# Reordering the front of a delta-rule layer: keys one group ahead, the first group by tiles, the rates as four pieces, the last queries turned by GpSimd

## The chip, the cores and the metric

The kernel runs on one core of one Trainium2 chip. The metric is the device time of one launch in microseconds. It is compared before and after the change, by the median of several executions of each kernel. The profile of the kernel before is one further execution.

## The reference

A vision tower of 32 images with 64 tokens each and width 256 passes through eight layers with a layer norm behind each: patch embedding and attention, a mixture of experts, a gated delta rule with 16 heads of 16, and further mixing, attention and expert layers. The change touches the delta layer alone:

```python
q = silu(x @ Wq).reshape(b, n, h, hd)
k = silu(x @ Wk).reshape(b, n, h, hd)
k = k * rsqrt(sum(k * k, -1, keepdims=True) + 1e-12)
v = (x @ Wv).reshape(b, n, h, hd)
beta = 2.0 * sigmoid(x @ Wbet)
a = sigmoid(x @ Wf)
def step(S, inp):                       # one of n = 64 steps
    Sd = at * S
    u = vt - einsum('bhk,bhkv->bhv', kt, Sd)
    Sn = Sd + bt * kt * u
    return Sn, einsum('bhk,bhkv->bhv', qt, Sn)
```

Here x is the layer norm of the expert layer's output. The steps can't begin before the keys and rates of all images are there, since one step works on all 32 images and 16 heads at once (512 chains, on 128 partitions in four groups).

## The kernel before, in words

The 2048 tokens are 16 tiles (T) of 128; four tiles (NT), which are eight images, make a group, and there are four groups (CG). Every engine has its own program; programs meet at semaphores. What stands between the end of the expert layer and the first step is called the front here.

- **Rows.** SyncE (`sync`) loads the two expert outputs of a tile into one of four buffers (`load_rows`, L1339); VectorE (`collect`, L1570 to L1583) adds them to H and takes the statistics; GpSimd (`rstd`, L1669) finishes them; ScalarE (`norm`, L1469) writes the normed tile; TensorE turns it (`turn`, through the helper at L108) and ScalarE copies it to xT (`copy_xT`, L1476).
- **Projections.** Six pieces of 128 features (0 and 1 are the queries, 2 and 3 the keys, 4 and 5 the values) fill PSUM banks 2 to 7, each from two matmuls over the 512 tokens of a group (L1388; the first group in two halves of 256 tokens, L1398). The 32 rates are one 32x512 sum in bank 1 (`rate_sums`, L1414), which the turns of odd tiles use too. A matmul in f32 runs as two instructions in the trace. ScalarE evicts with Silu or Copy (`made_of`, L1487) and the rates with Tanh (`rates_of`, L1497).
- **Change of layout.** Tokens lie along the free axis, but the steps need one chain to a partition: each piece is stored to DRAM (`store_made`, L1325, 1024 runs of 256 bytes) and a whole group of queries, keys or values is loaded back (`load_chain`, L1331). Keys and rates go and come by SyncE's queue; queries and values are stored by ScalarE's queue and loaded by GpSimd's.
- **Keys.** ScalarE squares a group of keys (`square_keys`, L1501), VectorE takes their norms by Newton steps and makes the scaled keys `ka` (`sum_keys`, `scale_keys`, L1595 to L1618), GpSimd makes `kb` (L1678). ScalarE turns the queries to time order (`turn_queries`, L1505).
- **Order.** TensorE and ScalarE follow `ticks`: a step with a lag of so many tiles, once per tile or per group. Per group TensorE does keys, rates, values, queries, one pair beside one turn. All stores and loads of keys on SyncE's queue stand behind all row loads. GpSimd takes the groups in order: values, queries, then `kb` of that group ahead of the next loads.
- **Steps.** Their program (L1635 on) begins when all pieces are stored, `kb` is made four times, the queries are turned, TensorE has cleared the states (L1454) and ScalarE has placed the values of the first step (L1508), which follows a load of its activation table. The 64 steps then run at VectorE's pace.

Of the kernel before, what the change touches and what calls it, by code (L numbers as in the profile page):

```python
# [16 lines left out]
F32 = mybir.dt.float32  # L17
# [1101 lines left out]
def vit_rest(nc, io, banks, H, ident, ident_bf, minus_half, const, const_in, scores_all, top, which, gate, xn_rows,  # L1119
             token_rows, spare):  # L1120
    chains = {n: nc.dram_tensor(f"chains_{n}", (CG, P, HD * TOK), F32).ap() for n in "qkvo"}
    rates = nc.dram_tensor("rates", (CG, 2, IMAGES // CG, HEADS, TOK), F32).ap()
    inter = nc.dram_tensor("inter", (T * GPT, ME, D), F32).ap()
# [112 lines left out]
def delta_front_buffers(nc, ctx):  # L1236

    def sb(name, shape, dt=F32):
        return ctx.enter_context(nc.sbuf_tensor(name, shape, dt))

    ng = IMAGES // CG * TOK
    return {"w": sb("w_delta", [P, DC, 3 * D]), "w_rate": sb("w_rate", [P, DC, 2 * HEADS]), "ys": sb("ys", [P, YS, 2, D]),
            "stats": [sb(f"stats_d{p}", [P, 6]) for p in range(2)], "agg": sb("agg_d", [P, T, 2]),
            "shift": sb("shift_d", [P, T]),
            "xT": [sb(f"xT_d{p}", [P, DC, ng]) for p in range(2)], "made": sb("made", [P, 6, ng]),
            "rate_made": sb("rate_made", [2 * HEADS, ng])}

# [14 lines left out]
def delta_layer(nc, sem, io, banks, H, ident, minus_half, token_rows, gate, chains, rates, front, chain, all_sent,  # L1262
# [50 lines left out]
    def rate_bank():  # L1313
        return banks[0:2 * HEADS, 1, :]

    def ticks(steps, last):
        for tick in range(last):
            for lag, per, count, step in steps:
                if tick >= lag and (tick - lag) % per == 0 and (tick - lag) // per < count:
                    step((tick - lag) // per)  # L1320

# [16 lines left out]
    def sync(sp):  # L1338
        def load_rows(t):  # L1339
            sp.dma_start(ys[t % YS][:, :, :], token_rows[0:2 * T * P, :]  # L1340
                         .rearrange("(k t p) d -> t p k d", k=2, p=P)[t]).then_inc(sem(f"ys{t % YS}"), 16)

        def next_rows(t):
            sp.wait_ge(sem("added"), t + 1)
            load_rows(t + YS)

        def send_keys(g):
            store_made(sp, g, 2)
            store_made(sp, g, 3)
            sp.wait_ge(sem("rate_made"), g + 1)  # L1350
            for kind in range(2):
                sp.dma_start(rates[g, kind, :, :, :].rearrange("b h t -> h b t"),
                             rate_made[kind * HEADS:(kind + 1) * HEADS, :].rearrange("h (b t) -> h b t", t=TOK)
                             ).then_inc(sem("rate_stored"), 16)
            load_chain(sp, g, "k", k)
            sp.wait_ge(sem("rate_stored"), 32 * g + 32)
            for kind in range(2):
                sp.dma_start(rate[:, g, kind, :], rates[g, kind, :, :, :].rearrange("b h t -> (b h) t")
                             ).then_inc(sem(f"rates{g}"), 16)

        all_sent(sp)
        for t in range(YS):
            load_rows(t)
        for t in range(T - YS):
            next_rows(t)
        for g in range(CG):
            send_keys(g)
        for g in range(CG):
            sp.wait_ge(sem(f"normed_o{g}"), 1)
            sp.dma_start(chains["o"][g], o[:, g, :, :].rearrange("p d t -> p (d t)")).then_inc(stored_o[g], 16)  # L1370

    def tensor(pe):
        def turn(t):
            if t >= 2:
                pe.wait_ge(sem("xT_copied"), t - 1)
            if t % NT == 1 and t > NT:
                pe.wait_ge(sem("rate_made"), t // NT)
# [3 lines left out]
        def project(first):  # L1381
            def step(g):
                pe.wait_ge(sem("xT_copied"), NT * g + NT)
                for m in (first, first + 1):
                    if g:
                        pe.wait_ge(sem(f"made{m}"), g)
                    for c in range(DC):
                        ins = pe.matmul(banks[:, 2 + m, :], w[:, c, m * P:(m + 1) * P], xT[g % 2][:, c, :],  # L1388
                                        start=(c == 0), stop=(c == 1))
                    ins.then_inc(sem(f"sums{m}"), 1)  # L1390
            return step

        def project_half(half, pieces):
            at = slice(half * NT // 2 * P, (half + 1) * NT // 2 * P)
            pe.wait_ge(sem("xT_copied"), (half + 1) * NT // 2)
            for m in pieces:
# [3 lines left out]
                if half:  # L1400
                    ins.then_inc(sem(f"sums{m}"), 1)

        def first_half(_):
            project_half(0, (2, 3, 4, 5, 0, 1))

        def second_half(first):
            def step(g):
                if g:
                    project(first)(g)
                else:  # L1410
                    project_half(1, (first, first + 1))
            return step

        def rate_sums(g):  # L1414
# [21 lines left out]
        def sum_squares(n, part):  # L1436
# [9 lines left out]
        ticks([(1, 1, T, turn), (3, 1, 1, first_half), (5, 4, CG, second_half(2)), (5, 4, CG, rate_sums),  # L1446
               (6, 4, CG, second_half(4)), (7, 4, CG, second_half(0))], T + 4)
        pe.wait_ge(sem("zeroed"), 1)
# [19 lines left out]
    def scalar(act):  # L1468
# [5 lines left out]
        def copy_xT(t):  # L1474
            act.wait_ge(sem("xT_made"), t + 1)
            g, i = t // NT, t % NT  # L1476
            if g >= 2 and i == 0:
                act.wait_ge(sem("sums5"), g - 1)
            act.copy(xT[g % 2][:, :, i * P:(i + 1) * P], turned_bank(t)).then_inc(sem("xT_copied"), 1)

        def made_of(first, func):
            def step(g):
                for m in (first, first + 1):
                    act.wait_ge(sem(f"sums{m}"), g + 1)
                    if g:
                        act.wait_ge(sem(f"stored{m}"), 16 * g)
                    act.activation(made[m][:, :], banks[:, 2 + m, :], func).then_inc(sem(f"made{m}"), 1)  # L1487
                if first != 2:
                    for m in (first, first + 1):
                        store_made(act, g, m)  # L1490
            return step

        def rates_of(g):
            act.wait_ge(sem("rate_sums"), g + 1)
            if g:
                act.wait_ge(sem("rate_stored"), 32 * g)
            act.activation(rate_made[:, :], rate_bank(), ACT.Tanh, scale=0.5).then_inc(sem("rate_made"), 1)  # L1497
# [21 lines left out]
        def square_out(n):  # L1519
            act.wait_ge(sem("o_made"), CUTS[n + 1])  # L1520
            if n:
# [3 lines left out]

        ticks([(0, 1, T, norm), (1, 1, T, copy_xT), (5, 4, CG, made_of(2, ACT.Silu)), (5, 4, CG, rates_of),
               (6, 4, CG, made_of(4, ACT.Copy)), (7, 4, CG, made_of(0, ACT.Silu)), (9, 4, CG, square_keys),
               (12, 4, CG, turn_queries)], T + 9)
        act.preload_act_table_set("natural_log_exp_and_others")
# [37 lines left out]
    def vector(dve):  # L1567
# [39 lines left out]
        def scale_keys(g):  # L1607
            dve.wait_ge(sem(f"rates{g}"), 32)
            once.mark(dve.tensor_scalar(rate[:, g, 1, :], rate[:, g, 1, :], 0.5, 0.5, ALU.mult, ALU.add))
# [23 lines left out]
        dve.wait_ge(sem("kb_made"), CG)  # L1633
        dve.wait_ge(sem("q_turned"), CG)
        dve.wait_ge(sem("values_placed"), 2)  # L1635
# [14 lines left out]
        for h in range(2):  # L1650
            dve.wait_ge(sem(f"state{h}"), TOK + 1)
        once.mark(dve.tensor_tensor(prod[:, :, :, 0:HD], S[TOK % 2], bcast(qt[:, last, :, :], 2, HD), ALU.mult))
        once.settle()
# [13 lines left out]
    def gpsimd(pool):  # L1667
# [16 lines left out]
        prepare(pool)  # L1684
        for g in range(CG):
            if g:
# [904 lines left out]
def laid_out_more(inputs, a, rows, wide, tok):  # L2591
# [12 lines left out]
    def columns(v):  # L2604
# [37 lines left out]
        "delta_w": rows(np.concatenate([a("L1_attn_Wq"), a("L1_attn_Wk"), a("L1_attn_Wv")], 1)),  # L2642
        "rate_w": rows(np.concatenate([a("L1_attn_Wbet"), a("L1_attn_Wf")], 1)),
        "delta_o_w": rows(a("L1_attn_Wo")),
# [82 lines left out]
```

## Time and profile before

| | us |
|---|---|
| median of 3 runs | 1377.79 (1375.93 to 1379.68) |
| the profiled execution's own time | 1378.83 |
| its span | 1377.2 |
| first collect of the front | 572.11 |
| first instruction of the steps (VectorE, L1640) | 659.93 |

TensorE is busy for 84% of the span, VectorE for 58%, ScalarE for 43% and GpSimd for 38%. These shares are means over very different stages. The front is 87.8 us long, and what counts in it is the chain of waits that ends at 659.93. In the rows further down, a line of the timeline has its start, its duration, the engine, the line of the kernel and the operation, and in brackets the engine's idle time before it and what ended that. "issue" there means that the engine's own sequencer was occupied.

### The profile page before, as it was taken

To read this page: it belongs to the slowest core of one execution; us is meant where nothing else is said; L and a number is where in the kernel's file an instruction comes from. 1 tells how busy PE (TensorE), PEld (TensorE's weight loads), DVE (VectorE), ACT (ScalarE), POOL (GpSimd) and SP (SyncE) were. 2 spreads that over 40 slices of the span, in tenths; PEclk is the share of its full clock that TensorE was granted. 3 is DMA by queue.
4 is the path that set the end of the run, shared out by engine and by line. 5 is a ranking of instruction groups with operands and counts; after the bars stand their busy time and mean duration, and the time that the engine had idled before them with its cause. 6 is when DMAs were issued, how large, how long until landed. Compare 5 with 4: busy or idle time off the path is not lost. (4 is left out here: it accounts for less than half of the span.)

```text
span 1377.2 us, 24939 instructions
## 1 busy us (share of the span) xinstructions
PE 1162.9 (84%) x9227; PEld 893.3 (65%) x9227; DVE 803.7 (58%) x1850; ACT 587.3 (43%) x1468; POOL 521.5 (38%) x565
## 2 busy tenths in 40 slices
PE   6999985699999999688689999994899999777854
PEld 4666663598999999543355656563677777655533
DVE  3666665321212121465899999994576776422886
ACT  2445542211121212155677777771244444334554
POOL 0111111232333323343688888882121222020657
PEclk9999996799999999899899999996899999878975
DMA  4111100799888887388000000002000040037601
GB/s 138 44 47 37 43 13 12 290 333 374 318 331 315 331 313 291 105 205 217 5 1 1 1 1 1 1 1 80 10 12 9 13 188 1 1 117 249 184 19 58
DMA packets 83353, 162.26 MB, mean 118 GB/s; under 512 B 44128, under 2 KB 62176, under 8 KB 77216
## 3 DMA queue, kind: packets, MB, share of 16 engines
q1 hardware_dynamic: 55536, 111.23, 23.6%
q0 software_dynamic: 10512, 45.10, 8.6%
q10 hardware_dynamic: 17184, 4.33, 1.5%
q8 instruction: 75, 1.23, 0.4%
q14 instruction: 46, 0.38, 0.1%
HBM read 134.28 MB, written 26.35 MB: 117 GB/s over the span
## 5 line engine op out<-in xcount | busy, mean ns | idle before, releaser
L922 PE MATMUL banks<-rowsT,w_up 128*128 128x128 f32 x1716 | 199.4, 276 | 0.0
L922 PEld LDWEIGHTS banks<-rowsT,w_up 128*128 128x128 f32 x1716 | 196.3, 193 | 0.1
L1431 PEld LDWEIGHTS banks<-ys,ident 128*128 128x128 f32 x1008 | 127.7, 191 | 99.8 <-POOL ys L1700 65.8
L1697 POOL TENSOR_TENSOR ys<-xT_d,q_by_time 128x1024 f32<-128x1024 f32 x63 | 149.2, 2368 | 42.6 <-ACT xT_d L1513 42.6
L1431 PE MATMUL banks<-ys,ident 128*128 128x64 f32 x1008 | 136.3, 291 | 21.8 <-POOL ys L1700 21.7
L1422 PE MATMUL banks<-made,ident 128*128 128x512 f32 x256 | 136.9, 617 | 14.5 <-DVE made L1645 14.4
L1542 ACT ACTIVATE banks<-banks,rate 128x256 f32<-128x256 f32 x256 | 104.0, 444 | 69.1 <-DVE made L1640 68.7
L936 PE MATMUL banks<-w_down,hT 128*128 128x256 f32 x468 | 107.5, 379 | 0.6 <-DVE res L1101 0.6
L1091 DVE TENSOR_TENSOR hT<-banks,silu 64x128 f32<-64x128 f32 x39 | 11.0, 283 | 165.6 <-ACT silu L979 165.6
L1643 DVE TENSOR_REDUCE banks<-made 128x32 f32<-128x544 f32 x128 | 93.2, 728 | 4.4
L864 POOL DMA_DIRECT2D w_down<-in_down_w x39 | 22.8, 585 | 186.5 <-PE banks L936 178.4
L936 PEld LDWEIGHTS banks<-w_down,hT 128*128 128x128 f32 x468 | 85.9, 190 | 11.0 <-issue 1.0
L1842 POOL TENSOR_TENSOR agg_b<-agg_b,minus_half 128x1 f32<-128x1 f32 x48 | 28.5, 593 | 170.0 <-DVE agg_b L2060 168.9
L1640 DVE TENSOR_TENSOR made<-banks,ka 128x512 f32<-128x512 f32 x128 | 87.6, 684 | 6.5 <-PE banks L1422 3.9
L1645 DVE TENSOR_TENSOR made<-kb,banks 128x512 f32<-128x512 f32 x128 | 88.0, 687 | 4.4
L1700 POOL TENSOR_TENSOR ys<-ys 128x512 f32<-128x512 f32 x63 | 79.3, 1258 | 4.9
L969 ACT COPY rowsT<-banks 128x256 f32<-128x256 f32 x39 | 14.5, 373 | 146.6 <-PE banks L108 146.6
L1513 ACT COPY xT_d<-banks 128x512 f32<-128x512 f32 x126 | 73.2, 581 | 0.0
L1101 DVE COPY res<-banks 128x256 f32<-128x256 f32 x39 | 16.6, 425 | 75.2 <-PE banks L936 75.2
L462 PE MATMUL banks<-w_tok,patches 128*128 128x256 f32 x192 | 51.2, 405 | 7.1 <-DMA patches<-in_patches 7.1
L2460 POOL TENSOR_TENSOR agg<-agg,minus_half 128x1 f32<-128x1 f32 x48 | 31.5, 657 | 60.6 <-DVE agg L2513 60.5
L454 POOL TENSOR_TENSOR ss<-ss,minus_half 128x1 f32<-128x1 f32 x16 | 8.8, 549 | 117.0 <-DVE ss L712 117.0
(313 smaller groups left out, 2350.5 us busy)
## 6 DMA issues: line engine op xcount, KB each, us to landing
w_up<-in_up_w SPq DMA_DIRECT2D x39, 1408.0 KB
w_down<-in_down_w POOLq DMA_DIRECT2D x39, 768.0 KB, 5.6
inter<-res_x SPq DMA_DIRECT2D x16, 512.0 KB, 3.1
back<-inter SPq DMA_DIRECT2D x15, 512.0 KB, 4.2
patches<-in_patches SPq DMA_DIRECT2D x16, 384.0 KB, 3.3
f<-in_f SPq DMA_DIRECT2D x6, 1024.0 KB, 10.7
ys<-token_rows SPq DMA_DIRECT2D x16, 256.0 KB, 2.8
xn_rows<-xn_all SPq DMA_DIRECT2D x16, 128.0 KB, 1.7
```

What stands on the lines that cost most here:

```text
L462: ins = pe.matmul(X, patches[t % SLOTS_IN][:, c, :], w_tok[:, c, :], start=(c == 0), stop=(c == PC - 1), skip_group_check=True)
L922: ins = pe.matmul(out[:, m * P:(m + 1) * P], w[:, c, m * P:(m + 1) * P], x[:, c, :], start=(c == 0), stop=(c == 1))
L936: ins = pe.matmul(Y, hT[j % 2][:, c, :], w_down[j % DEEP][:, c, :], start=(c == 0), stop=(c == FULL))
L1422: pe.matmul(S[(t + 1) % 2][:, halves[h], :, :], ident[:, :], outer[:, halves[h], :, :], start=False, stop=True, skip_group_check=True).the ...
L1431: ins = pe.matmul(o_sum[t % 2], ident[:, :], products[t % 2][:, :, :, n], start=(n == 0), stop=(n == FOLDED - 1))
L1513: act.copy(Sc[n % 2][:, halves[h], :, :], S[n % 2][:, halves[h], :, :]).then_inc(sem("state_copied"), 1)
L1542: ins = act.activation(S[(t + 1) % 2][:, g, :, :].rearrange("p v k -> p (v k)"), S[t % 2][:, g, :, :].rearrange("p v k -> p (v k)"), ACT.Copy,
L1640: dve.tensor_tensor(prod[:, at, :, 0:HD], S[t % 2][:, at, :, :], bcast(ka[:, t, at, :], 2, HD), ALU.mult).then_inc(sem(f"prod_made{h}"), 1)
L1643: dve.tensor_reduce(u[:, at, :], prod[:, at, :, :], AX.X, ALU.add).then_inc(sem(f"u_made{h}"), 1)
L1645: dve.tensor_tensor(outer[:, at, :, :], bcast(kb[:, t, at, :], 2, HD), bcast(u[:, at, :], 3, HD), ALU.mult).then_inc(sem(f"outer_made{h}"), 1)
L1697: pool.tensor_tensor(qs[:, :, :, :], Sc[(t + 1) % 2][:, :, :, :], bcast(qt[:, t, :, :], 2, HD), ALU.mult).then_inc(sem("qs_made"), 1)
L1700: pool.tensor_tensor(qs[:, :, :, 0:FOLDED], qs[:, :, :, 0:FOLDED], qs[:, :, :, FOLDED:2 * FOLDED], ALU.add).then_inc(sem("qs_folded"), 1)
```

## The change

What it does, engine by engine:

- **Order.** `ticks` is gone; TensorE's and ScalarE's orders are written out. TensorE: turn 0, turn 1, tile 0, turn 2, tile 1, turn 3, tile 2, turn 4, tile 3, turns 5 to 7, rates 0, keys 1, turns 8 and 9, piece 4 of group 1, turn 10, piece 5 of group 1, turn 11, rates 1, keys 2, turn 12, queries 1, rates 2, piece 4 of group 2, turns 13 and 14, piece 5 of group 2, turn 15, keys 3, rates 3, queries 2, values 3, queries 3.
- **First group.** Each of its four tiles is projected by itself (128 tokens, 24 matmul instructions) as soon as it is turned.
- **ScalarE.** Its end runs: copy 15, values 2, turn queries 0, keys 3, square keys 2, rates 3, queries 2, values 3, turn queries 1, queries 3, square keys 3, turn queries 2. `values(g)` still stores pieces 4 and 5 from ScalarE's queue.
- **Rates.** Their sum is four pieces of 32 rows and 128 columns, on partitions 0, 32, 64 and 96, so the eviction is 128x128 in place of 32x512. One store and one load for a group take the place of two and two.
- **SyncE.** The row loads of tiles 4 to 13 come first, then the keys of group 0, then the last two row loads. It stores the queries now, and loads the values and queries of group 3.
- **GpSimd.** It loads the other values and queries between the `kb` of the groups, and turns the queries of group 3 itself.

```diff
+        def store_rates(g):
             sp.wait_ge(sem("rate_made"), g + 1)
...
+            sp.dma_start(rates[g].rearrange("(b j) h n t -> (j h n) b t", b=2),
+                         rate_made[:, :].rearrange("p (b t) -> p b t", b=2)).then_inc(sem("rate_stored"), 16)
...
+        for t in range(10):
             next_rows(t)
-        for g in range(CG):
-            send_keys(g)
+        store_pair(keys, 0)
+        next_rows(10)
+        next_rows(11)
+        store_pair(queries, 0)
+        store_rates(0)
+        load_chain(sp, 0, "k", k)
+        load_rates(0)
+        store_pair(keys, 1)
...
+        store_pair(keys, 3)
+        store_rates(3)
+        store_pair(queries, 2)
+        load_chain(sp, 3, "k", k)
+        load_rates(3)
+        store_pair(queries, 3)
+        load_chain(sp, 3, "v", v)
+        load_chain(sp, 3, "q", q)
...
+        def project_tile(t):
+            at = slice(t * P, (t + 1) * P)
+            pe.wait_ge(sem("xT_copied"), t + 1)
+            for m in (2, 3, 4, 5, 0, 1):
...
+        def rate_sums(g, copied):
+            pe.wait_ge(sem("xT_copied"), copied)
+            if g:
+                pe.wait_ge(sem("rate_made"), g)
             for c in range(DC):
-                ins = pe.matmul(rate_bank(), w_rate[:, c, :], xT[g % 2][:, c, :], start=(c == 0), stop=(c == 1))
+                images = xT[g % 2][:, c, :].rearrange("p (b j t) -> p j b t", b=2, j=NT)
+                for j in range(NT):
+                    rows = slice(2 * HEADS * j, 2 * HEADS * (j + 1))
+                    ins = pe.matmul(rate_bank()[rows, :].rearrange("p (b t) -> p b t", b=2), w_rate[:, c, :],
+                                    images[:, j, :, :], start=(c == 0), stop=(c == 1), skip_group_check=True)
...
-        for g in range(CG):
-            if g:
-                scale_keys(g - 1)
-            load_chain(pool, g, "v", v)
-            load_chain(pool, g, "q", q)
-        scale_keys(CG - 1)
-        pool.wait_ge(sem("q_turned"), CG)
+        load_chain(pool, 0, "v", v)
+        load_chain(pool, 0, "q", q)
+        load_chain(pool, 1, "v", v)
+        scale_keys(0)
+        load_chain(pool, 1, "q", q)
+        scale_keys(1)
+        load_chain(pool, 2, "v", v)
+        scale_keys(2)
+        load_chain(pool, 2, "q", q)
+        scale_keys(3)
+        pool.wait_ge(sem(f"chain_q{CG - 1}"), 16)
+        pool.tensor_copy(qt[:, :, CG - 1, :].rearrange("p t d -> p d t"), q[:, CG - 1, :, :]
+                         ).then_inc(sem("last_turned"), 1)
```

## Rows read from the trace of the kernel before

**Rows 1.** Windows view: busy time and instructions per engine, granted clock, DMA share.

```profile
core 0: us, PE busy (x) PEld busy (x) DVE busy (x) ACT busy (x) POOL busy (x), PEclk, DMA share, GB/s
580.00:585.00 5.00, 5.00 (x16) 4.06 (x16) 4.62 (x15) 1.46 (x3) 2.61 (x7) 0.62 0.53 151
600.00:605.00 5.00, 4.54 (x8) 2.03 (x9) 0.61 (x3) 1.93 (x5) 3.16 (x7) 0.66 0.85 221
645.00:650.00 5.00, 4.22 (x11) 1.56 (x9) 2.99 (x7) 3.43 (x3) 3.73 (x1) 1.00 1.04 269
```

**Rows 2.** Timeline of TensorE in the front: start, duration, first to last group.

```profile
579.94 7.26 PE L1398 MATMUL banks<-xT_d,w_delta 128*128 128x256 f32 x24
...
600.46 0.41 PE L108 MATMUL banks<-ident,H 128*128 128x128 f32 x2 [2.97 <-ACT H L1471]
600.71 5.32 PE L1388 MATMUL banks<-xT_d,w_delta 128*128 128x512 f32 x8
605.96 1.90 PE L1416 MATMUL banks<-xT_d,w_rate 128*32 128x512 f32 x4
...
638.82 7.13 PE L1388 MATMUL banks<-xT_d,w_delta 128*128 128x512 f32 x16
```

**Rows 3.** Timeline of ScalarE: first copy, its stall, and the end of the front.

```profile
577.60 0.37 ACT L1479 COPY xT_d<-banks 128x256 f32<-128x256 f32 x1
...
599.72 0.60 ACT L1471 ACTIVATE H<-H,shift_d,agg_d 128x256 f32<-128x256 f32 x1 [1.53 <-issue]
...
637.10 0.60 ACT L1487 ACTIVATE made<-banks 128x512 f32<-128x512 f32 x1 [1.12 <-PE banks L1388]
...
646.00 0.60 ACT L1487 ACTIVATE made<-banks 128x512 f32<-128x512 f32 x1 [1.12 <-PE banks L1388]
...
648.82 1.06 ACT L1501 ACTIVATE chain_o<-chain_k 128x1024 f32<-128x1024 f32 x1
655.83 2.00 ACT L1505 COPY q_by_time<-chain_q 128x1024 f32<-128x1024 f32 x1 [5.95 <-DMA chain_q<-chains_q]
657.84 1.28 ACT L1529 ACT_TABLE_LOAD   x1
659.13 0.39 ACT L1508 COPY made<-chain_v 128x32 f32<-128x32 f32 x2
```

**Rows 4.** Timeline of VectorE: first and last collect, keys of group 3, first step.

```profile
600.53 0.15 DVE L1583 TENSOR_SCALAR agg_d<-agg_d 128x1 f32<-128x1 f32 x1
...
649.91 1.87 DVE L1595 TENSOR_REDUCE n<-chain_o 128x64 f32<-128x1024 f32 x1 [1.87 <-ACT chain_o L1501]
...
655.47 1.94 DVE L1618 TENSOR_TENSOR ka<-chain_k,f 128x1024 f32<-128x1024 f32 x1
659.93 0.69 DVE L1640 TENSOR_TENSOR made<-banks,ka 128x512 f32<-128x512 f32 x1 [2.52 <-ACT made L1508]
```

**Rows 5.** Timeline of GpSimd: the last load of queries, `kb`, the first product.

```profile
650.76 0.55 POOL L1331 DMA_DIRECT2D chain_q<-chains_q  x1
655.64 3.87 POOL L1678 TENSOR_TENSOR kb<-chain_k,f 128x1024 f32<-128x1024 f32 x1 [4.33 <-DVE f L1616]
668.78 2.35 POOL L1697 TENSOR_TENSOR ys<-xT_d,q_by_time 128x1024 f32<-128x1024 f32 x1 [9.28 <-ACT xT_d L1513]
```

**Rows 6.** Timeline of SyncE's issues for the last keys.

```profile
636.00 2.09 SPq L1325 DMA_DIRECT2D chains_k<-made  x2
...
643.51 0.34 SPq L1331 DMA_DIRECT2D chain_k<-chains_k  x1
```

**Rows 7.** TensorE's groups by shape: count | busy us, mean ns | idle before.

```profile
L922 PE MATMUL banks<-rowsT,w_up 128*128 128x128 f32 x1716 | 199.4, 276 | 0.0
...
L936 PE MATMUL banks<-w_down,hT 128*128 128x256 f32 x468 | 107.5, 379 | 0.6 <-DVE res L1101 0.6
...
L255 PE MATMUL banks<-w_qkv,hT 128*64 128x128 f32 x256 | 18.4, 288 | 0.0
...
L2311 PE MATMUL banks<-back,perm_t 128*32 128x256 f32 x128 | 12.0, 452 | 9.6 <-issue 8.2 <-DMA back<-inter 1.4
```

More of the change, by code:

```diff
@@ L1121, in vit_rest @@
     chains = {n: nc.dram_tensor(f"chains_{n}", (CG, P, HD * TOK), F32).ap() for n in "qkvo"}
-    rates = nc.dram_tensor("rates", (CG, 2, IMAGES // CG, HEADS, TOK), F32).ap()
+    rates = nc.dram_tensor("rates", (CG, IMAGES // CG, HEADS, 2, TOK), F32).ap()
     inter = nc.dram_tensor("inter", (T * GPT, ME, D), F32).ap()
@@ L1313, in rate_bank @@
     def rate_bank():
[L1314 to L1320, printed above, removed]
+        return banks[:, 1, 0:P]
     def store_made(queue, g, m):
@@ L1345, in next_rows, with store_pair, load_rates @@
             load_rows(t + YS)
-        def send_keys(g):
-            store_made(sp, g, 2)
-            store_made(sp, g, 3)
+        def store_pair(first, g):
+            store_made(sp, g, first)
+            store_made(sp, g, first + 1)
+        def store_rates(g):
             sp.wait_ge(sem("rate_made"), g + 1)
[L1351 to L1359, printed above, removed]
+            sp.dma_start(rates[g].rearrange("(b j) h n t -> (j h n) b t", b=2),
+                         rate_made[:, :].rearrange("p (b t) -> p b t", b=2)).then_inc(sem("rate_stored"), 16)
+        def load_rates(g):
+            sp.wait_ge(sem("rate_stored"), 16 * g + 16)
+            sp.dma_start(rate[:, g, :, :].rearrange("p n t -> p (n t)"),
+                         rates[g].rearrange("b h n t -> (b h) (n t)")).then_inc(sem(f"rates{g}"), 16)
+        queries, keys = 0, 2
         all_sent(sp)
@@ L1363, in sync @@
             load_rows(t)
-        for t in range(T - YS):
+        for t in range(10):
             next_rows(t)
-        for g in range(CG):
-            send_keys(g)
+        store_pair(keys, 0)
[6 more added lines that the diff above has]
+        store_pair(keys, 1)
+        store_rates(1)
+        load_chain(sp, 1, "k", k)
+        load_rates(1)
+        store_pair(keys, 2)
+        store_rates(2)
+        store_pair(queries, 1)
+        load_chain(sp, 2, "k", k)
+        load_rates(2)
+        store_pair(keys, 3)
[6 more added lines that the diff above has]
+        load_chain(sp, 3, "q", q)
         for g in range(CG):
@@ L1375, in turn, with turn_past_rates, project @@
                 pe.wait_ge(sem("xT_copied"), t - 1)
-            if t % NT == 1 and t > NT:
-                pe.wait_ge(sem("rate_made"), t // NT)
             pe.wait_ge(sem("ln_done"), t + 1)
             transposes(pe, turned_bank(t), H[:, t, :], ident[:, :], DC).then_inc(sem("xT_made"), 1)
[L1381 to L1384, printed above, removed]
-                    if g:
[L1386 to L1396, printed above, removed]
+        def turn_past_rates(t, g):
+            pe.wait_ge(sem("rate_made"), g + 1)
+            turn(t)
+        def project(m, g):
+            pe.wait_ge(sem("xT_copied"), NT * g + NT)
+            if g:
+                pe.wait_ge(sem(f"made{m}"), g)
+            for c in range(DC):
+                ins = pe.matmul(banks[:, 2 + m, :], w[:, c, m * P:(m + 1) * P], xT[g % 2][:, c, :],
+                                start=(c == 0), stop=(c == 1))
+            ins.then_inc(sem(f"sums{m}"), 1)
+        def project_tile(t):
+            at = slice(t * P, (t + 1) * P)
+            pe.wait_ge(sem("xT_copied"), t + 1)
+            for m in (2, 3, 4, 5, 0, 1):
                 for c in range(DC):
@@ L1399, in project_half @@
                                     start=(c == 0), stop=(c == 1), skip_group_check=True)
-                if half:
+                if t == NT - 1:
                     ins.then_inc(sem(f"sums{m}"), 1)
[L1403 to L1414, printed above, removed]
-            for c in range(DC):
-                ins = pe.matmul(rate_bank(), w_rate[:, c, :], xT[g % 2][:, c, :], start=(c == 0), stop=(c == 1))
+        def rate_sums(g, copied):
+            pe.wait_ge(sem("xT_copied"), copied)
+            if g:
+                pe.wait_ge(sem("rate_made"), g)
+            for c in range(DC):
+                images = xT[g % 2][:, c, :].rearrange("p (b j t) -> p j b t", b=2, j=NT)
[3 more added lines that the diff above has]
+                                    images[:, j, :, :], start=(c == 0), stop=(c == 1), skip_group_check=True)
             ins.then_inc(sem("rate_sums"), 1)
@@ L1445, in tensor @@
         pe.wait_ge(sem("weights"), 32)
-        ticks([(1, 1, T, turn), (3, 1, 1, first_half), (5, 4, CG, second_half(2)), (5, 4, CG, rate_sums),
-               (6, 4, CG, second_half(4)), (7, 4, CG, second_half(0))], T + 4)
+        turn(0)
+        turn(1)
+        project_tile(0)
+        turn(2)
+        project_tile(1)
+        turn(3)
+        project_tile(2)
+        turn(4)
+        project_tile(3)
+        turn(5)
+        turn(6)
+        turn(7)
+        rate_sums(0, 8)
+        project(2, 1)
+        project(3, 1)
+        turn(8)
+        turn_past_rates(9, 0)
+        project(4, 1)
+        turn(10)
+        project(5, 1)
+        turn(11)
+        rate_sums(1, 12)
+        project(2, 2)
+        project(3, 2)
+        turn(12)
+        project(0, 1)
+        project(1, 1)
+        rate_sums(2, 12)
+        project(4, 2)
+        turn_past_rates(13, 2)
+        turn(14)
+        project(5, 2)
+        turn(15)
+        project(2, 3)
+        project(3, 3)
+        rate_sums(3, 16)
+        project(0, 2)
+        project(1, 2)
+        project(4, 3)
+        project(5, 3)
+        project(0, 3)
+        project(1, 3)
         pe.wait_ge(sem("zeroed"), 1)
@@ L1476, in copy_xT, with evict, queries, keys @@
             g, i = t // NT, t % NT
-            if g >= 2 and i == 0:
-                act.wait_ge(sem("sums5"), g - 1)
-            act.copy(xT[g % 2][:, :, i * P:(i + 1) * P], turned_bank(t)).then_inc(sem("xT_copied"), 1)
[L1481 to L1491, printed above, removed]
+            if t == 2 * NT:
+                act.wait_ge(sem("rate_sums"), 1)
+            if t == 3 * NT:
+                act.wait_ge(sem("rate_sums"), 2)
+                act.wait_ge(sem("sums1"), 2)
+            act.copy(xT[g % 2][:, :, i * P:(i + 1) * P], turned_bank(t)).then_inc(sem("xT_copied"), 1)
+        def evict(first, g, func):
+            for m in (first, first + 1):
+                act.wait_ge(sem(f"sums{m}"), g + 1)
+                if g:
+                    act.wait_ge(sem(f"stored{m}"), 16 * g)
+                act.activation(made[m][:, :], banks[:, 2 + m, :], func).then_inc(sem(f"made{m}"), 1)
+        def queries(g):
+            evict(0, g, ACT.Silu)
+        def keys(g):
+            evict(2, g, ACT.Silu)
+        def values(g):
+            evict(4, g, ACT.Copy)
+            store_made(act, g, 4)
+            store_made(act, g, 5)
         def rates_of(g):
@@ L1524, in square_out @@
                        o[:, :, :, CUTS[n]:CUTS[n + 1]]).then_inc(sem("o_squared"), 1)
-        ticks([(0, 1, T, norm), (1, 1, T, copy_xT), (5, 4, CG, made_of(2, ACT.Silu)), (5, 4, CG, rates_of),
-               (6, 4, CG, made_of(4, ACT.Copy)), (7, 4, CG, made_of(0, ACT.Silu)), (9, 4, CG, square_keys),
-               (12, 4, CG, turn_queries)], T + 9)
+        norm(0)
+        norm(1)
+        copy_xT(0)
+        norm(2)
+        copy_xT(1)
+        norm(3)
+        copy_xT(2)
+        norm(4)
+        copy_xT(3)
+        norm(5)
+        copy_xT(4)
+        norm(6)
+        keys(0)
+        copy_xT(5)
+        norm(7)
+        copy_xT(6)
+        copy_xT(7)
+        values(0)
+        rates_of(0)
+        queries(0)
+        norm(8)
+        norm(9)
+        keys(1)
+        copy_xT(8)
+        copy_xT(9)
+        norm(10)
+        norm(11)
+        copy_xT(10)
+        norm(12)
+        copy_xT(11)
+        values(1)
+        rates_of(1)
+        norm(13)
+        norm(14)
+        keys(2)
+        square_keys(0)
+        norm(15)
+        copy_xT(12)
+        rates_of(2)
+        queries(1)
+        copy_xT(13)
+        copy_xT(14)
+        square_keys(1)
+        copy_xT(15)
+        values(2)
+        turn_queries(0)
+        keys(3)
+        square_keys(2)
+        rates_of(3)
+        queries(2)
+        values(3)
+        turn_queries(1)
+        queries(3)
+        square_keys(3)
+        turn_queries(2)
         act.preload_act_table_set("natural_log_exp_and_others")
@@ L1607, in scale_keys @@
         def scale_keys(g):
-            dve.wait_ge(sem(f"rates{g}"), 32)
+            dve.wait_ge(sem(f"rates{g}"), 16)
             once.mark(dve.tensor_scalar(rate[:, g, 1, :], rate[:, g, 1, :], 0.5, 0.5, ALU.mult, ALU.add))
```

12 lines of the change are left out of this document (7 added, 5 removed).

## The prediction

> **What bounds the kernel now.** I read the page's shares first and set them aside, since the change touches one stage. Then I read the windows of that stage [rows 1], the timelines of TensorE and ScalarE [rows 2, 3], those of VectorE and GpSimd [rows 4, 5], SyncE's issues [rows 6] and TensorE's groups by shape [rows 7]. The reader is to see four things.
>
> VectorE has added and measured all 16 tiles by 600.68 [rows 4], but TensorE starts the keys of group 1 at 600.71 only, and the last query sums are evicted from 646.00 [rows 2, 3]. So after 600 TensorE's queue is the bound of the front, not the rows or the norms.
>
> That queue holds waste. The clock is at its lower level for much of 580 to 585 (0.62 granted, of which 1.2 GHz would be 0.50) and again in 600 to 605 (0.66) [rows 1]. The second spell follows an idle time of 2.97 us that ended in a norm of ScalarE, and ScalarE itself had stood 1.53 us at "issue" behind its two stores of queries [rows 2, 3]. Eight instructions took 5.32 us there; sixteen took 7.13 later, 3.57 for eight [rows 2].
>
> Behind TensorE comes a tail. The sums of the last keys are evicted at 637.10; store and load bring them back for the squares at 648.82 [rows 3, 6]; VectorE works from 649.91, GpSimd's `kb` runs from 655.64 to 659.51, and the steps begin at 659.93 [rows 4, 5].
>
> A second tail ends in the same 0.5 us: the last queries land at 655.83, ScalarE turns them for 2.00, loads its table for 1.28 and places values until 659.52 [rows 3].
>
> What follows the first step is unchanged, at VectorE's pace, so I carry any shift of 659.93 to the end at full size.
>
> **The change, part by part.**
>
> *First group by tiles.* The first copy to xT ends at 577.97 [rows 3]; TensorE then works on tile 0, where before it began two tiles at 579.94 [rows 2]. Four tiles are 4 x 24 = 96 instructions of 128x128. The expert layer's same shape took 199.4/1716 = 0.116 us each [rows 7], so 11.1 us, and a turn costs 0.25 (600.46 to 600.71) [rows 2], three of them 0.8. If the clock rises when it did before (0.62 over 5 us is 3.8 us at the lower level, until 583.8) [rows 1], the 5.8 us from 577.97 do 2.9 us of that work. The remaining 9.0 end at 592.8. Turns 5 to 7, with two copies of 0.37 that they wait for, make it 594.1.
>
> *Rates in four pieces.* Before, four instructions of 128x512 took 1.90 us [rows 2]. Now there are 16 of 128 columns for each group, on four column blocks of 32. The trace has no such instruction. One bound is no overlap at all: 16 x 0.116 = 1.9. The other comes from the 32-column form L2311, 12.0/128 = 0.094 for 256 columns, or 0.047 for 128: 0.75. The 64-column form L255 gives 18.4/256 = 0.072, hence 1.15 [rows 7]. Both forms run below what a serial instruction of their length takes, so blocks do overlap. I take 1.0, between the latter two, which saves 0.9 per group. The Trainium skill (TensorEngine Tiling (Array Packing), Key Properties and Theoretical Speedup) says that column tiles load weights and multiply independently, up to four times as fast, while a change of mode drains the engine. A full factor of four would make the sum of a group about 0.5 and the end 0.5 x 4 = 2 us earlier; the trace's 32-column row shows well under 4, against 107.5/468 = 0.23 for a full 256-column instruction (0.094 against 0.23 is 2.4 times at most) [rows 7].
>
> The eviction goes from 32x512 (about 0.6) to 128x128, and one store and one load of rates go per group. All of it is beside TensorE's work: nothing on the path. A dearer rates transfer (below 1 us either way) would hide behind the keys' own, whose load is later.
>
> *Keys one group ahead.* Rates 0 end at 595.1 and the keys of group 1 start there, against 600.71: 5.6 us earlier. Beyond that, the slow spell (5.32 - 3.57 = 1.75 us) is gone if the clock stays up; TensorE's longest wait in the new order is about 0.7 us.
>
> From there to the last sum stand 18 pieces at 1.72 (the spacing of evictions, 0.60 + 1.12) [rows 3], 31.0; three rates, 3.0; eight turns, 2.0; and the copies behind turns 11 and 15, which the next sum needs whole, 0.45 each, with 0.3 for the rest: 37.2. The last query sums are there at 632.3, against 646.00. The last keys have rates 3 and six pieces behind them, 11.3 us, so they are there at 621.0, against 637.10: 16.1 us earlier.
>
> *The tail after it.* Store and load took 637.10 to 643.51 and 643.51 to 648.82, 11.7 us in all [rows 3, 6]. So the last keys are back at 632.7. ScalarE has `queries(3)` ahead of the squares: evicted from 632.3 and done at about 632.9, squares end at 633.9 (632.3 + 1.6). From the squares' end (649.88) to the first step it was 10.05 us [rows 3, 4]; the first step is then at 643.95.
>
> *SyncE's queue.* The stores of queries move from ScalarE to SyncE, eight issues; on ScalarE the pairs of groups 1 to 3 go as well as that of group 0. In front of the last keys' load stand the queries of group 2: evicted until 621.0 + 1.0 + 3.4 + 0.6 = 626.0, when the keys' store is not yet down (621.0 + 6.4 = 627.4). So the added wait costs nothing by 1.4 us. Ahead of it, the queries of group 0 hold the load of keys 0 by some 2 us; their squares stand behind keys 2 on ScalarE anyway.
>
> *Moved row loads.* The loads of tiles 14 and 15 follow the first keys' eviction (about 591) and land before VectorE comes to tile 14 at 597: nothing. Bounds: 0 to 1.8 us on the last norms, which ScalarE now runs after 605.
>
> *Last queries on GpSimd.* A copy of 128x1024 isn't in its rows. Bounds are 1.06 (ScalarE's square of that size) and 3.87 (`kb`, also with a permuted output) [rows 3, 5]; I take 2.35, as for its product of 128x1024. The queries of group 3 land at about 643.5, and GpSimd's first product came 8.85 us after the first step [rows 4, 5]. Even 3.87 is hidden; with it gone from ScalarE, 2.0 us leave the second tail.
>
> *What is late next.* Two chains stand close. GpSimd loads the queries of group 2 only after `kb` 2. Squares 0 follow keys 2, about 609.6; VectorE needs 7.5 us a group (649.91 to 657.41), so `kb` 2 ends near 634.1; load 0.6 and 5.1 to land, turn 2.0, table 1.28, values 0.39: 643.6. VectorE's four groups alone give `kb` 3 at 641.7. So a still faster TensorE would bring under 1 us more.
>
> **Sum.** 659.93 - 643.95 = 16.0 us. I take off 2.0. ScalarE still issues the stores of values 0 in the middle of the front, where a pair stalled it 1.53 [rows 3], and the last keys' return and the queries' eviction now meet to 0.1 us, so that any lateness of either counts. The gain forecast is 14.0 us. The profiled execution took 1378.83, which gives 1364.8; the median of the runs shown is 1.04 lower, which gives 1363.8. I predict 1364.3.
>
> **Rivals.**
>
> *R1, the transfers become the bound.* The DMA engines' share is 0.85 to 1.04 already in such windows [rows 1]; the same bytes now have to move in 14 us less. For: the last keys' way has two transfers in a row with no slack. Against: the bytes near the end are spread, as the queries of group 2 go earlier than values 3. If each landing is 2 to 4 us later, the first step is 4 to 8 later than 643.95 plus part of the 2.0: gain 6 to 10, 1368 to 1372.
>
> *R2, more than the sum.* The clock rises 1 to 2 us earlier and the stall of 2.0 doesn't come: gain 16 to 18, where the chain of queries 2 ends it: 1360 to 1362.
>
> *R3, slower: the clock stays low.* The waits behind turns 7, 11 and 15 and short matmuls might let the clock fall as after the 2.97 us. The price: work at the lower level takes twice its time. All of the 37.2 us from the keys of group 1 on would add 37.2 and make it 21 us slower, 1400; it decides from 16 us of such work. Against it: from 645 to 650 TensorE stood 0.78 us and the clock was granted at 1.00 [rows 1]; the fall came after it had stood 2.97 [rows 2].
>
> *R4, the change doesn't do what it says.* The reordering could move the end of TensorE's queue but not the first step, where stored pieces, values and the table gate it: within 4 us of before.
>
> **Numbers.** Forecast (gain 11 to 16) 0.67; R1 0.19; R2 0.07; R3 0.03; R4 0.04. What a measurement can tell from no change is about 0.3%, 4.1 us. Faster by more: 0.67 + 0.19 + 0.07 = 0.93. Within: 0.04. Slower: 0.03. The range reaches from R2's middle to R1's middle: 1360.5 to 1371.
>
> **What would show it.** Right: TensorE's keys of group 1 near 595 at full clock; last sums near 632 to 634; the first step near 646, with VectorE, GpSimd and ScalarE all ready within 2 us; rates at 0.8 to 1.2 us. Wrong: a granted clock below 0.9 after 595 (R3); squares of group 3 that wait on the keys' landing by over 2 us (R1); a first step that is held by ScalarE's values while `kb` is long done; or steps that run slower than before.

## The result and the profile after

| | before | after |
|---|---|---|
| median, 11 runs each (us) | 1378.42 (1373.52 to 1384.47) | 1367.94 (1361.27 to 1376.49) |
| ratio | | 0.9924 (0.9900 to 0.9948) |
| profiled execution (us) | 1378.83 | 1373.86 |
| front: first collect to first step (us) | 87.82 | 74.70 |
| first step to last store of o (us) | 287.2 | 287.2 |
| behind that, to the end (us) | 430.1 | 435.6 |

The change is 10.5 us faster (7 to 14 by the interval); 1364.3 was predicted and the range held. The front of the profiled execution is 13.1 us shorter, against 14.0 forecast. What doesn't fit is behind it: there the changed code is the same and this execution was 5.5 us slower. The experiments come back to that.

TensorE's timeline of the changed kernel, columns as in [rows 2]:

```profile
580.73 5.18 PE L1414 MATMUL banks<-xT_d,w_delta 128*128 128x128 f32 x24
...
596.75 0.65 PE L1427 MATMUL banks<-xT_d,w_rate 128*32 128x128 f32 x16 [0.46 <-ACT xT_d L1534]
597.33 3.70 PE L1405 MATMUL banks<-xT_d,w_delta 128*128 128x512 f32 x8
...
622.69 0.64 PE L1427 MATMUL banks<-xT_d,w_rate 128*32 128x128 f32 x16
623.26 10.57 PE L1405 MATMUL banks<-xT_d,w_delta 128*128 128x512 f32 x24
```

The front began at 574.74 here (572.11 before), so subtract. The keys of group 1 start 22.6 us into the front (28.6 before), the last keys' sums are there at 47.9 (65.0), the last sums at 59.1 (73.8). Of the two low-clock spells of [rows 1] the second is gone (1.00 granted from 600 to 605, 0.66 before); the first is still there (0.50 from 580 to 585). ScalarE's and GpSimd's ends of the front:

```profile
628.23 0.26 ACT L1558 ACTIVATE rate_made<-banks 128x128 f32<-128x128 f32 x1
...
635.05 0.60 ACT L1541 ACTIVATE made<-banks 128x512 f32<-128x512 f32 x1 [0.56 <-DMA chains_q<-made]
638.45 1.06 ACT L1562 ACTIVATE chain_o<-chain_k 128x1024 f32<-128x1024 f32 x1 [1.49 <-DMA chain_k<-chains_k]
643.03 1.94 ACT L1566 COPY q_by_time<-chain_q 128x1024 f32<-128x1024 f32 x1 [3.53 <-DMA chain_q<-chains_q]
```

```profile
637.91 0.58 POOL L1325 DMA_DIRECT2D chain_q<-chains_q  x1
...
645.28 3.82 POOL L1792 TENSOR_TENSOR kb<-chain_k,f 128x1024 f32<-128x1024 f32 x1 [6.79 <-DVE f L1729]
649.06 1.91 POOL L1810 COPY q_by_time<-chain_q 128x1024 f32<-128x1024 f32 x1
```

From 635 to its last turn, every idle time of ScalarE ends in a DMA, where [rows 3] had TensorE. SyncE's queue, and windows with the DMA share in the column before the last (columns as in [rows 1]; the first row is the whole front before, the second the whole front after):

```profile
624.09 1.28 SPq L1319 DMA_DIRECT2D chains_k<-made  x2
628.51 0.36 SPq L1347 DMA_DIRECT2D rates<-rate_made  x1
629.00 1.32 SPq L1319 DMA_DIRECT2D chains_q<-made  x2
630.41 2.01 SPq L1325 DMA_DIRECT2D chain_k<-chains_k  x1
```

```profile
572.11:659.93 87.82, 62.63 (x176) 30.50 (x176) 54.38 (x148) 42.90 (x71) 37.13 (x47) 0.89 0.75 192
574.74:649.44 74.70, 57.21 (x272) 33.48 (x272) 54.35 (x149) 38.51 (x70) 34.55 (x46) 0.89 0.85 226
...
625.00:630.00 5.00, 5.00 (x13) 2.28 (x12) 3.44 (x2) 2.68 (x5) 3.73 (x3) 1.00 1.14 331
630.00:635.00 5.00, 3.83 (x9) 1.33 (x7) 4.49 (x17) 2.55 (x2) 0.87 (x1) 1.00 1.13 280
```

In windows of 5 us the share is 0.92 or more from 595 to 640. The last keys' load took 8.0 us from issue to squares, 5.3 before [rows 3, 6]. The difference in landing is larger still: before, the load had landed 4.3 us after its issue (647.85), and ScalarE came to the squares 1.0 us later, behind its turn of queries 2; after, it took 8.0 to land. The share around the two was 1.04 [rows 1] and 1.13. The first step is at 649.44, released by `kb`, 9.93 us behind the end of the squares (10.05 before).

### The profile page after: what moved, and what is told of

Read it like the earlier page. It is cut to its first block and busy times, and to the rows that moved or that the text cites. A ratio compares the mean times of both kernels' runs of the same rounds, so it can differ in the third digit from the quotient of the medians.

```text
span 1372.2 us, 25136 instructions
## 1 busy us (share of the span) xinstructions
PE 1168.4 (85%) x9323; PEld 904.7 (66%) x9323; DVE 803.3 (59%) x1850; ACT 582.3 (42%) x1467; POOL 519.2 (38%) x564
## 5 line engine op out<-in xcount | busy, mean ns | idle before, releaser
L922 PE MATMUL banks<-rowsT,w_up 128*128 128x128 f32 x1716 | 202.5, 279 | 1.9 <-DMA w_up<-in_up_w 1.9
L922 PEld LDWEIGHTS banks<-rowsT,w_up 128*128 128x128 f32 x1716 | 199.2, 196 | 2.2 <-DMA w_up<-in_up_w 2.1
L864 POOL DMA_DIRECT2D w_down<-in_down_w x39 | 22.6, 579 | 190.8 <-PE banks L936 182.7
```

Source lines behind the costliest of these rows:

```text
L922: ins = pe.matmul(out[:, m * P:(m + 1) * P], w[:, c, m * P:(m + 1) * P], x[:, c, :], start=(c == 0), stop=(c == 1))
```

## The experiments

A front is read from one profile each, a time from 4 to 12 runs. The changed kernel's own two fronts differ by 0.7 us. "Load" is the issue of the last keys' load, "squares" the start of their squares, both in us from the first collect; "landed" is the time from that issue to the landing. "Held by" names what released the first step; in before, `kb` and the values ended within 0.02 us of each other. Ratios are to the kernel before on the same chip.

| kernel | load | landed | squares | TensorE's last sum | front | held by | ratio (interval) |
|---|---|---|---|---|---|---|---|
| before | 71.40 | 4.3 | 76.71 | 73.84 | 87.82 | values | |
| after | 55.67 | 8.0 | 63.71 | 59.09 | 74.70 | kb | 0.9924 (0.9900, 0.9948) |
| again | 55.37 | 7.6 | 63.00 | 59.14 | 73.99 | kb | 0.9890 (0.9858, 0.9922) |
| rates3_first | 54.76 | 10.0 | 64.74 | 58.61 | 75.73 | kb | 0.9925 (0.9900, 0.9950) |
| scalar_turn | 56.32 | 7.2 | 63.59 | 58.75 | 76.06 | values | 0.9904 (0.9875, 0.9933) |
| scalar_stores | 54.56 | 6.0 | 62.97 | 60.38 | 73.96 | kb | 0.9890 (0.9857, 0.9923) |
| light | 55.67 | 6.1 | 61.82 | 59.11 | 73.10 | values | 0.9903 (0.9873, 0.9932) |
| late_v2 | 54.65 | 6.4 | 61.10 | 58.47 | 74.22 | values | 0.9901 (0.9869, 0.9934) |
| halves | 58.27 | 6.7 | 65.03 | 61.81 | 78.81 | values | 0.9903 (0.9873, 0.9933) |
| whole_rates | 57.72 | 6.1 | 63.98 | 63.46 | 74.98 | kb | 0.9928 (0.9900, 0.9956) |
| pool_turns | 56.10 | 4.9 | 61.06 | 59.06 | 72.05 | kb | 0.9896 (0.9863, 0.9930) |
| pool_turns_ss | 54.02 | 5.4 | 61.23 | 60.10 | 72.24 | kb | 0.9900 (0.9869, 0.9930) |
| before_rates4 | 68.01 | 3.9 | 72.22 | 69.34 | 83.42 | kb | 0.9980 (0.9959, 1.0001) |
| order_only | 61.53 | 6.6 | 68.15 | 65.73 | 80.89 | values | 0.9947 (0.9925, 0.9969) |

**again**: no edit.

> The changed kernel once more. In its first profile the front (first collect of VectorE to first step) took 74.70 us against 87.82 before, 13.1 shorter, while the span from the first step on was 5.5 us longer (mean granted clock 0.84 against 0.86 in the last layers). Theory N (what is outside the front is the spread of executions): the front is 74 to 75.5 again, the steps to the last store of o 287.2 again, and the stretch behind them lies anywhere from 428 to 437 with its granted clock, so the time differs from the kernel before by 10 to 15 us. Rival S (the earlier front systematically costs something later): the stretch behind the last store of o is again 435 or more.

The front is 73.99, the stretch behind the last store of o 429.5 in place of 435.6, the median 1363.76 against 1378.58. Over the 14 profiles that stretch, whose code nobody touched, lies between 424.5 and 435.6, with no order by kernel (424.7 in scalar_stores, 430.1 before). So the 5.5 us are spread and not a price of the change; theory N holds. Slower runs go in the main with a lower clock: of the changed kernel's 11, those at a mean grant of 0.927 took 1361.27 and 1363.81, that at 0.916 took 1373.86 and that at 0.877 took 1376.49.

**rates3_first**

```diff
-        square_keys(2)
         rates_of(3)
+        square_keys(2)
```

> ScalarE's order alone: the last rates are evicted before the squares of group 2. In the changed kernel they waited behind those squares until 628.23, SyncE stood at their store (624.09 + 1.28 to 628.51), and the load of the last keys was issued at 630.41 and took 8.0 us to the squares. Theory Q (SyncE's queue held by the rates makes the last keys late): the store of rates goes at about 625.5, the load of keys is issued about 1 us earlier, the front is 0.5 to 1.5 us shorter. Rival D (the DMA engines are full, share 1.13 there, so the landing is set by bytes in flight): the keys land at the same time within 0.4 us, and the front stays at 74.7.

The load left 0.6 to 0.9 us earlier and its keys were squared 1.0 to 1.7 us later, 9.98 us after the issue. Leaving earlier bought nothing, which is against Q. D is missed too: it had the landing within 0.4 us and the front at 74.7, and both came 1 us or more later (75.73). This is one profile, and why the load took 10.0 us stays open.

**scalar_turn**

```diff
-        pool.tensor_copy(qt[:, :, CG - 1, :].rearrange("p t d -> p d t"), q[:, CG - 1, :, :]
...
+        turn_queries(3)          # on ScalarE, behind turn_queries(2)
```

> The last queries are turned by ScalarE again, the rest is the changed kernel. There ScalarE placed the first values until 646.68 and kb 3 ended at 649.10; the last queries landed before 649.06. The prediction's working: the second tail gets 2.0 us longer and waits for their landing. If they land at about 647.5, turn 2.0, table 1.3, values 0.4 put the first step at 651.5, so the front is 2 us longer (76.5 to 77). Rival: they land early enough (644.5) and the first step stays with kb at 74.7.

76.06, 1.4 to 2.1 longer, and the release has changed from `kb` to ScalarE's values, as expected:

```profile
642.54 2.34 ACT L1566 COPY q_by_time<-chain_q 128x1024 f32<-128x1024 f32 x1 [0.44 <-DMA chain_q<-chains_q]
```

**scalar_stores**

```diff
-        store_pair(queries, 0)   # and 1, 2, 3, on SyncE
...
+            store_made(act, g, 0)
+            store_made(act, g, 1)
```

> The queries are stored from ScalarE's queue again, the rest is the changed kernel. Theory Q (what one issuer's queue holds up is what counts): ScalarE stands 1 to 2 us at each pair (it stood 1.40, 1.65 and 1.51 behind values 1, 2 and 3), SyncE loses 8 issues of about 0.8 us, and the last keys' load goes about 1 us earlier but ScalarE comes to its squares later; the front within 1 us of 74.7 on either side. Rival D (the 16 DMA engines are the bound, whichever queue issues): no difference over 0.5 us. Rival B: ScalarE's stalls reach TensorE as they did before (2.97 us idle, low clock) and the front is 3 us longer or more.

73.96, in the reach of Q as of D. The trace tells more than the front. The keys' load left 0.8 to 1.1 us earlier and landed 6.0 us after its issue (7.6 and 8.0 in the changed kernel), so the last keys were back 2.4 to 3.1 us earlier. But ScalarE was at its own two stores of queries then and came to the squares 2.4 us after the landing, "issue" ahead of them and no DMA:

```profile
636.24 2.47 ACTq L1319 DMA_DIRECT2D chains_q<-made  x2
638.75 1.06 ACT L1560 ACTIVATE chain_o<-chain_k 128x1024 f32<-128x1024 f32 x1 [1.96 <-issue]
```

So the front is the same because a gain and a loss cancel, as Q had it, and not because the issuer makes no difference to the landing, as D had it. Whether the load landed sooner because no stores of queries stood ahead of it in SyncE's queue, no run separates. ScalarE's stalls did reach TensorE, whose last sum is 1.2 us later, but not by the 3 us of rival B.

**light**: the loads of queries 1 and values 2 carry an eighth of their bytes. The kernel leaves out the rest, so what it computes is no longer the layer.

```diff
+        part = 16 if (n, g) in (("q", 1), ("v", 2)) else P
...
-        queue.dma_start(dst[:, g, :, :].rearrange("p d t -> p (d t)"), chains[n][g]
+        queue.dma_start(dst[0:part, g, :, :].rearrange("p d t -> p (d t)"), chains[n][g][0:part, :]
```

> The changed kernel, but the loads of queries 1 and of values 2, which are in flight beside the last keys, carry 16 of 128 partitions (64 KB in place of 512 KB); the rest of those two pieces is zero, filled by two VectorE memsets in its idle time. In two profiles of the changed kernel the squares of the last keys started 8.04 and 7.63 us after their load was issued, with the DMA engines' share at 1.13; before it was 5.31. Theory D (bytes in flight set the landing): about 0.9 MB less takes 3 us of DMA time at 280 to 330 GB/s out of 622 to 638; the squares of keys 3 start 5.5 to 6.5 us after the issue, the front is 1 to 2 us shorter (72 to 73.5). Rival Q (one issuer's order sets it): unchanged, 74 to 74.7.

The load left at the same 55.67 and took 6.15 us, not 8.04 or 7.63: what flies beside it adds 1.5 to 1.9 us to its landing, D. The squares came 1.2 to 1.9 earlier and the front gained 0.9 to 1.6; the last 0.3 went to ScalarE's values, held by queries 2.

**late_v2**

```diff
-        load_chain(pool, 2, "v", v)
         scale_keys(2)
+        load_chain(pool, 2, "v", v)
```

> GpSimd's load of values 2 goes behind kb 2, so its 512 KB leave the time of the last keys' way (it was issued at 628.86, the keys' load at 630.41) and come 7 us later. Theory D: the last keys land about 1 us earlier, queries 2 and values 2 later; ScalarE's queries 2 may land at 44 instead of 43, still ahead of kb 3; the front is 0.5 to 1.3 us shorter than 74.0 to 74.7. Rival Q: no change. It is longer only if the queries of group 2 come so late that the placing of the values ends after kb 3.

The same bytes later: squares at 61.10, 1.9 to 2.6 earlier, and the front is unchanged. The second tail has taken over, the wait for queries 2 now 8.20 us long (3.53 after):

```profile
641.55 1.93 ACT L1566 COPY q_by_time<-chain_q 128x1024 f32<-128x1024 f32 x1 [8.20 <-DMA chain_q<-chains_q]
```

**halves**

```diff
-        project_tile(0)          # to 3, each behind the next turn
...
+        project_half(0)          # behind turn 2; project_half(1) behind turn 4
```

> The first group is projected in two halves of 256 tokens again, the rest is the changed kernel. The prediction's working: the tiles let TensorE begin with 24 instructions one tile earlier, at the low clock; by it the keys of group 1 start 1.5 to 2.5 us later here and the front is as much longer, 75.5 to 77. Theory D (the DMA engines bound the end): what TensorE loses here comes back in part, since the bytes get more room: the front is under 1 us longer.

78.81, 4.1 to 4.8 longer, beyond both. TensorE's keys of group 1 start 2.2 later and its last sum is 2.7 later. By `kb` alone, which ended at 75.87 (74.36 and 73.66 in the changed kernel), the front would be 1.5 to 2.2 longer, much as the prediction's working has it. The rest comes by the other tail, and it looks like a collision. In the changed kernel SyncE's store of keys 1 went ahead of GpSimd's two big loads (604.53; 606.20 and 606.87) and was down by 609.64. Here it went with them (604.33; 604.06 and 604.72) and held ScalarE's next keys until 614.05:

```profile
604.06 0.66 POOL L1325 DMA_DIRECT2D chain_v<-chains_v  x1 [0.30 <-POOL arena L1163]
...
640.89 0.58 POOL L1325 DMA_DIRECT2D chain_q<-chains_q  x1
```

```profile
604.33 1.07 SPq L1319 DMA_DIRECT2D chains_k<-made  x2
...
614.04 0.33 SPq L1325 DMA_DIRECT2D chain_k<-chains_k  x1
```

```profile
647.55 1.93 ACT L1564 COPY q_by_time<-chain_q 128x1024 f32<-128x1024 f32 x1 [8.86 <-DMA chain_q<-chains_q]
```

Squares 0 stand behind these keys on ScalarE, so `kb` 0 to `kb` 2 were late, and with them GpSimd's load of queries 2 (68.3 us into the front, 63.2 after). ScalarE waited 8.86 us for it, and its values held the first step. No run moved the store alone, so the collision is argued from the order of the rows, here and in order_only.

The ratio (0.9903) doesn't show those 4 us; four runs have an interval of 0.6% and can't.

**whole_rates**: the rates' sum, eviction, stores and loads as before.

```diff
-                for j in range(NT):
-                    rows = slice(2 * HEADS * j, 2 * HEADS * (j + 1))
+                ins = pe.matmul(rate_bank(), w_rate[:, c, :], xT[g % 2][:, c, :], start=(c == 0), stop=(c == 1))
...
```

> The rates are one sum of 32x512 again with two stores and two loads a group, the rest is the changed kernel. In the changed kernel 16 instructions of a group take 0.65 us (0.58 to the next start), before four took 1.90. The prediction's working: 1.3 us per group, so the last sums come 5 us later and the front is 5 us longer (79 to 80). Theory D: the last keys' way then has room (landing 6 us after the issue, not 8) and gives back 2: the front is 2 to 4 us longer.

TensorE's last sum is 4.3 us later, the front 0.3 to 1.0: D, and stronger than I had put it. The load left 2.1 to 2.3 later and took 6.26 to the squares.

**pool_turns**: late_v2, and

```diff
-        turn_queries(2)          # ScalarE
...
+        for g in (CG - 2, CG - 1):
+            pool.wait_ge(sem(f"chain_q{g}"), 16)
+            pool.tensor_copy(qt[:, :, g, :].rearrange("p t d -> p d t"), q[:, g, :, :]
```

> The changed kernel with the load of values 2 behind kb 2 (as in late_v2) and queries 2 turned by GpSimd as well, behind kb 3. In late_v2 the squares of the last keys started 61.10 us into the front in place of 63.00 and 63.71, but ScalarE turned queries 2 only when they had landed, and its values held the first step (4.56 us of VectorE's waiting): 74.22. Theory (two tails of equal length behind a full DMA): with that turn gone, the first step follows kb 3 at 61.1 + 10.0 = 71.1, so the front is 71 to 72, 2 to 3 us shorter than the changed kernel, and the time 2 us less. Rival: ScalarE's values still hold it, since values 3 land as late: 73.5 or more.

The front is 72.05, 1.9 to 2.7 shorter, and `kb` releases it again. Its own row shows the values ready 3.5 us ahead of the first step at 644.79:

```profile
640.88 0.39 ACT L1569 COPY made<-chain_v 128x32 f32<-128x32 f32 x2 [4.73 <-DMA chain_v<-chains_v]
```

The median (1363.71) doesn't tell it from the changed kernel's (1363.76 in again). The gain is shown in the profile and unresolved in the time.

**pool_turns_ss**: pool_turns with the edit of scalar_stores.

> pool_turns with the queries stored from ScalarE's queue. scalar_stores alone had a front of 73.96 against 73.99 and 74.70, its last keys' load issued 1 us earlier (54.56) and landed 8.4 us later. Theory D (full DMA engines, whoever issues): as pool_turns within 0.7 us. Rival Q (SyncE's queue counts): 1 us shorter than pool_turns, 70 to 71.

72.24, the same front as D had it. But as in scalar_stores the last keys were back earlier (59.4, against 61.0 in pool_turns) and waited for ScalarE, which evicted and stored queries until the squares at 61.23.

**before_rates4**: the kernel before with the rates' part of the change.

> The kernel before with one part of the change alone: the rates in four pieces, one store and one load a group. Before, TensorE was the bound of the front, with four rate sums of 1.9 us on its path; 1.3 us less in each of four groups, of which the last sits before the last queries but behind the last keys. Theory T (there TensorE still binds, so its time counts): last keys 3.9 us earlier, front 3.5 to 4.5 us shorter than 87.8. Rival D (the DMA engines bind there too): under 1.5 us shorter, as the same saving brought under 1 in the changed kernel.

83.42, 4.4 shorter: where TensorE binds, its 4.5 us (73.84 to 69.34) come out whole, theory T. The time moved by 0.2% (0 to 0.4). Together with whole_rates this is one saving under two bounds: 4.4 us in one order, 1.0 or less in the other.

**order_only**: the edits of halves, whole_rates and scalar_turn together.

> The written-out orders alone: the changed kernel with halves, whole rates and the last queries turned by ScalarE. The prediction's sum without the parts: tiles 2, rates 5, turn 0 to 2 us, so a front of 81 to 84. Theory D (the DMA engines' bytes set the end once TensorE is below them): TensorE's losses of 7 us come back in part; whole rates alone cost 0.3 to 1.0, scalar turn 1.4 to 2.1: a front of 77 to 79, and nearly all of the gain kept by the order.

80.89, just under the prediction's sum (81 to 84) and 1.9 over what D had. The order alone is worth 6.9 us, and the other three parts together 6.2 to 6.9; undone one by one they cost 5.8 to 7.9. I had taken for granted that a full DMA hides what is added; but here too keys 1 were stored with GpSimd's loads (stored at 607.37, loads from 606.95), and squares 0 came at 42.44, as in halves (41.94) and not as in the rest of the new orders (35 to 38).

## Why the prediction was right

Its times are put here as us from the first collect, and those measured are of after and again.

- **Order and tiles.** Keys of group 1 at 23.0; measured 22.6. Last keys' sums at 48.9; 47.9 and 47.9. Last sums at 60.2; 59.1 and 59.1. The walk along TensorE's queue, the larger part of the sum, held within 1.1 us.
- **Rates.** 1.0 a group was mis-sized: 0.58 to the next start, below the bound of 0.75 from L2311 [rows 7], and below the 0.8 to 1.2 given as a sign of being right. Before, it was 1.83 to the next start (636.99 to 638.82), so 3.2 times as long. The Trainium skill (TensorEngine Tiling (Array Packing), Theoretical Speedup) states up to four times for 32 columns; the trace comes near that.
- **The last keys' return** is the step that failed: "Store and load took [...] 11.7 us in all" was carried over. From the sums to the squares it was 15.8 and 15.1: 7.1 and 7.0 until the store was down (6.4 before), 0.6 and 0.5 until SyncE issued the load, and 8.0 and 7.6 until that had landed (4.3 before, and 1.0 more until ScalarE was free). The squares of keys 3 end at 64.8 and 64.1, not 61.8. light and late_v2 show that 1.2 to 1.9 us of the load's time come from what flies beside it; the rest isn't separated. The total came near since two things covered most of it: the sums were 1.0 early, for the rates' surplus, and 2.0 had been taken off. That 2.0 was for ScalarE's store issues and for any lateness of the keys' return; only the second shows in the front, about twice as large, so the near hit is in part luck.
- **R1** named the mechanism, "the last keys' way has two transfers in a row with no slack"; it was real, and I gave it 0.19 as if it were all or nothing. Its sign, squares that wait on the landing by over 2 us, reads 1.49 here, because ScalarE's evictions of the last queries, just ahead, waited for a store of queries first (0.56 and 0.71), which the sum didn't have.
- **ScalarE's rates 3** stood behind squares 2, which waited for keys 2: a wait that the prediction didn't see. rates3_first shows that it costs nothing here.
- **Row loads:** nothing, as predicted; no run tests it alone.
- **SyncE's stores of queries:** the working was wrong. "So the added wait costs nothing by 1.4 us" had the keys' store down last. In fact it was down 0.6 and 0.5 us before the load left, held by those stores, and with them on ScalarE the last keys were back 2.4 to 3.1 us earlier (scalar_stores). The front came out the same only because ScalarE lost that time itself.
- **The last queries on GpSimd:** hidden as predicted, 1.91 us against 2.35; undone it costs 1.4 to 2.1, against the 2.0 taken from the second tail.
- **What is late next:** the queries 2 chain at ScalarE, as said; late_v2 ran into it.
- **R3 and R4** didn't occur; the granted clock is 1.00 from 590 to 635.

The measured time's distance from 1364.3 (3.6 us) is within what the unchanged stretch behind varies by. The second sample had 1363.76.

## What to carry to other kernels

When a change packs a stage tighter, sum the transfers' busy time of that stage once against the new length: here some 66 us of DMA work (a share of 0.75 of 88 us) met 75, where the share was 0.92 or more for 45 us on end, and the landing time of the last keys, 4.3 us in the looser trace, became 8.0 and 7.6. When a change of queue leaves the time as it was, look at the landing too: a gain can hide behind an engine that isn't ready for it. A saving is worth its size only on the engine that binds: test it once in each order. And a profile of one stage resolves about 1 us (two of the changed kernel differ by 0.7) where the whole program's median over a handful of runs can't.

## What the runs showed that I had not expected

- Sixteen 128-column matmul instructions on four column blocks of 32 take 0.65 us, 0.041 each, where a full-width one of 128 columns takes 0.116 [rows 7].
- Where one pair of stores (512 KB) slipped by 1.9 us, from ahead of two 512 KB loads to beside them, it was down 9.7 us after its issue and not 5, and squares 0 came 5 to 6 us later (halves against the changed kernel, order_only likewise). That the one causes the other is argued and not shown.
- The last keys landed 1.6 to 3.1 us earlier when ScalarE's queue stored the queries, in both orders where this was tried, and neither front gained from it.
